# Indirect transfers of 126 rows in place of 125 in a graph network on one core: all five passes, the surplus row skipped

## The reference, cut to what matters

```python
edge_index = jnp.stack([src, dst])
h = relu(layernorm(x))
x = x + spline_conv(h, edge_attr_2, weight, root_w, root_b, edge_index)   # messages from h[src], summed at dst, mean over the degree, + h @ root_w.T + root_b
h = relu(layernorm(x))
x = x + gat_layer(h, edge_index, ...)   # 8 heads, softmax over the edges into a node and its self loop, then an MLP of 128, two layer norms
```

## Time and profile before

| what | us |
|---|---|
| median of 3 runs | 3404.45 (3403.78 to 3404.93) |
| the profiled execution | 3409.07 |
| its span, first to last instruction | 3406.9 |
| GpSimd busy | 2542.2 (75%), 2011 instructions |
| TensorE busy | 2036.6 (60%) |
| VectorE busy | 2020.0 (59%) |
| ScalarE busy | 789.4 (23%) |

### The profile page before, as it was taken

One profiled execution on the slowest core, in us unless ns is written; L12 is line 12 of the kernel. 1 busy time (PEld: TensorE's weight loads), 2 busy tenths in 40 slices (PEclk: granted clock), 3 DMA queues, 4 the chain that ended last, 5 costly groups with the idle time before them and its releaser, 6 DMA issues.

```text
span 3406.9 us, 31556 instructions
## 1 busy us (share of the span) xinstructions
PE 2036.6 (60%) x8829; PEld 1383.9 (41%) x8829; DVE 2020.0 (59%) x3417; ACT 789.4 (23%) x1511; POOL 2542.2 (75%) x2011
## 2 busy tenths in 40 slices
PE   2877777737776654564555065464461587887740
PEld 1554454525554443443443053353341244444420
DVE  5788878885666454444533034333348998798720
ACT  1332222213333221222222021121121022223210
POOL 8788888888888788887787777888850038888877
PEclk9888888877777776776676565566565788798765
DMA  2322222221212111111111011111110001111100
GB/s 57 85 70 70 67 71 65 46 64 31 50 39 53 32 36 34 41 34 29 35 29 29 11 24 21 27 25 22 23 17 0 30 15 23 37 27 27 33 10 10
DMA packets 116041, 123.16 MB, mean 36 GB/s; under 512 B 70597, under 2 KB 72618, under 8 KB 115941
## 3 DMA queue, kind: packets, MB, share of 16 engines
q0 software_dynamic: 64000, 30.57, 9.4%
q1 hardware_dynamic: 51940, 91.52, 8.4%
HBM read 59.51 MB, written 64.00 MB: 36 GB/s over the span
## 4 chain that ended last, share of the span: by engine, by line
POOL 67%; issue 19%; DVE 7%; PE 5%; ACT 0%; DMA 0%; POOLq 0%; DVEq 0%; ACTq 0%
POOL ring L411 45%; POOL x_table L433 14%; POOL out_rows L459 9%; DVE region L1443 2%; PE C L527 1%; PE V L745 1%; DVE region L1435 1%; PE V L515 1%; DVE region L1419 1%; DVE region L1101 1%; DVE region L1371 0%; DVE region L1394 0%; DVE region L1391 0%; PE C L745 0%; PE T L745 0%
## 5 line engine op out<-in xcount | busy, mean ns | idle before, releaser
L411 POOL DMA_INDIRECT ring<-in_x,index x800 | 1044.7, 1306 | 244.3 <-issue 243.7
L459 POOL DMA_INDIRECT out_rows<-ring,index_out x400 | 507.7, 1269 | 370.3 <-DVE ring L1242 250.0
L411 POOL DMA_INDIRECT ring<-x_table,index x400 | 494.0, 1235 | 124.4 <-issue 124.4
L433 POOL DMA_INDIRECT x_table<-region,index_out x400 | 492.8, 1232 | 121.9 <-issue 121.6
L476 PE MATMUL T<-ident,hrow 125*128 125x125 f32 x1000 | 198.9, 338 | 487.9 <-DVE hrow L1086 285.3
L527 PE MATMUL C<-w_c,hid 128*125 128x32 f32 x2400 | 354.9, 314 | 211.2 <-ACT hid L826 191.7
L1060 DVE TENSOR_REDUCE var<-sq 125x16 f32<-125x512 f32 x325 | 220.7, 682 | 375.8 <-ACT sq L810 284.4
L527 PEld LDWEIGHTS C<-w_c,hid 128*125 128x125 f32 x2400 | 351.2, 237 | 216.0 <-ACT hid L826 196.1
L515 PE MATMUL V<-xT,w_q 128*128 128x500 f32 x600 | 391.2, 809 | 63.8 <-ACT xT L802 38.7
L476 PEld LDWEIGHTS T<-ident,hrow 125*128 125x128 f32 x1000 | 150.4, 182 | 529.6 <-DVE hrow L1086 264.9
L1080 DVE TENSOR_REDUCE var<-ring 125x16 f32<-125x512 f32 x50 | 34.2, 684 | 497.1 <-DMA ring<-x_table,index 299.5
(11 more groups left out here) (229 smaller groups left out, 3192.3 us busy)
## 6 DMA issues: line engine op xcount, KB each, us to landing
ring<-in_x,index POOLq DMA_INDIRECT x800
nodes<-in_x SPq DMA_DIRECT2D x25, 500.0 KB
x_table<-nodes SPq DMA_DIRECT2D x25, 500.0 KB
x_plain<-nodes SPq DMA_DIRECT2D x25, 500.0 KB
nodes<-x_plain SPq DMA_DIRECT2D x50, 250.0 KB
out_rows<-nodes SPq DMA_DIRECT2D x50, 250.0 KB
x_table<-region,index_out POOLq DMA_INDIRECT x400
ring<-x_table,index POOLq DMA_INDIRECT x400
```

The lines of the kernel that those rows point to most:

```text
L411: pool.indirect_dma_start(out=ring[0:P, j, s * F:(s + 1) * F], out_offset=None, in_=table, in_offset=bass.IndirectOffsetOnAxis(ap=index[0: ...
L433: pool.indirect_dma_start(out=x1_table[:, :], out_offset=bass.IndirectOffsetOnAxis(ap=index_out[0:P, j, s:s + 1], axis=0), in_=rows_out[0: ...
L459: pool.indirect_dma_start(out=out[:, :], out_offset=bass.IndirectOffsetOnAxis(ap=index_out[0:P, j, s:s + 1], axis=0), in_=ring[0:P, j, s * ...
```

## The change

Every indirect transfer gets a 126th row. Its index is N, out of range, so nothing is moved for it; the gathers get the same bounds check that the scatters have. The indices of partition 125 on are set by VectorE at the start, `index` and `index_out` from partition 96 on (the loads and copies write partitions 0 to 124 over it later), and so is the part of `region2` from which row 125 of the scatters is addressed. `root_b` goes into rows 125 to 127 of `ring`, ahead of the first index load in SP's queue; GpSimd waits for it before its first gather and SP waits for the two index fills before its first index load. The centring of rows in SBUF by VectorE (`centre_rows`) is in the kernel before and stays as it is.

```diff
-N_BOOT = 6 * 4 + 2 + 2 + 2 + 4
+N_BOOT = 6 * 4 + 2 + 2 + 2 + 3
...
+ROWS = 126
...
+        index_set = sem("index_set"); root_b_in = sem("root_b_in")
...
+            sp.dma_start(ring[P:128, :, :].rearrange("a j (s f) -> a (j s) f", f=F),
+                         root_b.rearrange("(a b f) -> a b f", a=1, b=1).to_broadcast([128 - P, NJ * CE, F])).then_inc(root_b_in, 16)
+            sp.wait_ge(index_set, 2)
             for j in range(NJ):
                 index_load(src, 0, j, None)
...
-            load(ring[P:P + 1, :, :].rearrange("a j (s f) -> a (j s) f", f=F),
-                 root_b.rearrange("(a b f) -> a b f", a=1, b=1).to_broadcast([1, NJ * CE, F]))
...
             def gather(table, j):
...
-                        out=ring[0:P, j, s * F:(s + 1) * F], out_offset=None, in_=table,
-                        in_offset=bass.IndirectOffsetOnAxis(ap=index[0:P, j, s:s + 1], axis=0)).then_inc(ring_dma[j], 16)
+                        out=ring[0:ROWS, j, s * F:(s + 1) * F], out_offset=None, in_=table,
+                        in_offset=bass.IndirectOffsetOnAxis(ap=index[0:ROWS, j, s:s + 1], axis=0),
+                        bounds_check=last_row, oob_is_err=False).then_inc(ring_dma[j], 16)
...
+            pool.wait_ge(root_b_in, 16)
             gather_phase(x[:, :], 0, 0)
...
-                        out=x1_table[:, :], out_offset=bass.IndirectOffsetOnAxis(ap=index_out[0:P, j, s:s + 1], axis=0),
-                        in_=rows_out[0:P, j, s * F:(s + 1) * F], in_offset=None,
+                        out=x1_table[:, :], out_offset=bass.IndirectOffsetOnAxis(ap=index_out[0:ROWS, j, s:s + 1], axis=0),
+                        in_=rows_out[0:ROWS, j, s * F:(s + 1) * F], in_offset=None,
...
+            pool.wait_ge(index_set, 2)
...
-                            out=out[:, :], out_offset=bass.IndirectOffsetOnAxis(ap=index_out[0:P, j, s:s + 1], axis=0),
-                            in_=ring[0:P, j, s * F:(s + 1) * F], in_offset=None,
+                            out=out[:, :], out_offset=bass.IndirectOffsetOnAxis(ap=index_out[0:ROWS, j, s:s + 1], axis=0),
+                            in_=ring[0:ROWS, j, s * F:(s + 1) * F], in_offset=None,
...
+            v.memset(index[96:128, :, :], N).then_inc(index_set, 1)
+            v.memset(index_out[96:128, :, :], N).then_inc(index_set, 1)
+            v.memset(region2[96:128, 5904 + KS * GF:2 * H * TE + NJ * W], 0.0)
             dve.sem_inc(c_done, CREDIT)
```

## The result

The changed kernel takes 3898.07 us (3890.69 to 3907.39, 4 runs) against 3404.69 for the kernel before: 1.145 times as long, 95% interval 1.142 to 1.1475. I had forecast 2836.

A forecast was written before the change was run, and what follows sets the result against it. GpSimd's queue of 2,000 indirect transfers was taken to bound the kernel. From 3409.1, 492 saved through stage D and 78 in E, plus 2 for boot, gave 2841, or 2836 as median; range 2720 to 3200, chance 0.79.

The forecast's parts named there:

- VectorE keeps its times: Stage E, scatters to the output: VectorE's times stay, the last scatter lands at 3326 instead of 3404, 78 us saved.
- can go at 34.5: Stage B, dst gathers and x1 scatters: 34.5 us a chunk instead of 49.1, once VectorE no longer waits for the ring.
- VectorE's 118 a block: Stage A, first gathers: VectorE bounds at about 118 us per five-chunk block instead of 133.2, saving 60 us.
- my 0.83: Indirect transfer's instruction on GpSimd: 0.83 us instead of 1.21, the middle between 0.44 (all steps) and 1.21 or 1.22.
- my own table: Whole-kernel times for other instruction durations: 0.44 to 0.6 us gives 2745, 0.7 2775, 0.9 2925, 1.0 3055, 1.1 3205.
- Stage D: Gathers from the x1 table: 25 chunks take 464 us, ending at 2035 instead of 2527.5; 492 us saved in all.
- Rival 2: Transfer cost goes by rows, or by engines with rows: 1.22 us by rows, 3426 us in all; chance 0.10.
- slower: Whole kernel slower than before by over 0.2%: chance 0.10, against 0.85 for faster and 0.05 for the same.
- My signs of being wrong: Instruction over 1.0 us, the 0.30 us gap growing, or stage B above 40 us a chunk with GpSimd waiting.
- The gap of 0.30: Time on GpSimd between one indirect transfer and the next: stays 0.30 us, for a period of 1.13.
- The packets: Last stretch of scatters: 14 large and 18 small packets for each transfer, against 5 large and 27 small before.
- The bounds check: New on the gathers only; costed at nothing, at worst 0.02 us each, 24 us where GpSimd bounds.

The follow-up runs named there:

- 112 rows: Changed kernel with transfers of 112 rows, 7 on each of 16 engines, the rows beyond not moved: 3018.66 us on chip 5, 4060.79 on chip 8.
- 85 and 119 rows: Two changed kernels with 17 rows on each of 5 or 7 engines, rows beyond not moved, ring zeroed: 3350.48 and 3343.50 us.
- 49 rows: Changed kernel with transfers of 49 rows, 7 on each of 7 engines, the rows beyond not moved: 3077.82 us on chip 5, 3927.66 on chip 8.
- 105: Changed kernel with transfers of 105 rows, 7 on each of 15 engines, the rows beyond not moved: 3962.09 us on chip 3.
- 121 rows: Changed kernel with transfers of 121 rows, 11 on each of 11 engines, rows beyond not moved, ring zeroed: 3663.84 us.
- my first series: Changed kernel with fewer rows per transfer (85, 119, 121), rows beyond not moved, ring zeroed: 3350.48, 3343.50 and 3663.84 us.

## Why the prediction was wrong

*The step that failed* is in the working of the stages: "VectorE keeps its times", B that "can go at 34.5", A at VectorE's 118 a block. I took the pace of the other engines from rows in which GpSimd went at 1.51 us, and let it stand at 1.13. On the chips of the result their pace depends on GpSimd's: below a period somewhere between 1.47 us, where nothing is late, and 1.41 or 1.39, where it begins, TensorE's signals reach ScalarE and VectorE late, by 1 to 2.4 us on the mean in whole kernels. The instruction alone, 1.0 to 1.07 us in place of my 0.83, would by my own table have given 3055 to 3205 (112 rows, the nearest kernel without late signals, took 3019). By that estimate 690 to 840 us of the 3898 are this step. The second layer and the convolution are chains of short steps between TensorE and those two, so each delay is on the path. It feeds back: the late engines give `ring` and indices late, GpSimd waits (B's 391 us), and in its pauses the signals are prompt. So a shorter instruction buys GpSimd nothing. Stage D shows it best: its mean period is 1.43 to 1.55 us in every late kernel, against 1.54 before, though the median goes down to 1.29.

*Was this in the rows before?* No row of it showed a late signal, and none of my rivals had it. Rival 2, the one on the slower side, had "14 engines cost more to serve than 5", but at the price of GpSimd's own instruction, which did fall. So the 0.10 that I gave to "slower" would have been right by luck and not by its reason. My signs of being wrong did catch it: B is at 52 us a chunk (1300/25) with GpSimd waiting, and the instruction is above 1.0 us.

*The transfer.* The mechanism was right and its size off. Steps count: (1.190 - 0.987)/16 = 0.0127 us each for the scatter. But 25 of them are 0.32 of the 1.19 us; the other 0.87 is fixed. 17 steps took 1.082, 11 took 1.024 and 7 took 0.942 to 0.964, within 0.02 of that line, and 85 and 119 rows, both of 17 steps, took the same time, so it is the steps and not the rows. I had taken the middle of the bounds, 0.83, and the scatter measured 0.987, the gather 1.071. The gap of 0.30 held. The Trainium skill, "DMA: Bandwidth & Descriptors", section "Anatomy of one DMA — SWDGE (gpsimd) path", has the descriptors as a small part. By these runs they are about a quarter of the instruction at 125 rows: less than the half of my middle, but not nothing. The scatter came out about halfway between my 0.83 and the unchanged 1.19 of that rule. The packets fell out as expected from the divisor: 32 for each transfer still, and in the last stretch (3800 to 3880 us, 49 transfers) 14 large and 18 small.

*The bounds check* was costed at nothing or 0.02 us. It is 0.06 on each gather (72 us in all), and 0.078 in D at 126 rows, there with the skipped row. The scatters, on which I based it, have it in both kernels, so their equal time could not tell.

*The rest of the sum* can be judged where the signals are prompt. On chip 5 VectorE is 95% busy in stage A (381.77 of 400), and 400 gathers take 562 us, 22.5 a chunk where I had put 23.6. B, from first scatter to D, takes 955; my own steps with its period of 1.27 (gathers 1.29, scatters 1.25) give 847 + 720 x 0.14 = 948. D's gathers take 521 against 25 x 16 x 1.33 = 532. My table gave 3055 for an instruction of 1.0 us; 112 rows (0.99 and 0.94) took 3019, 49 rows (1.03 and 0.955) 3078. By that table 126 rows would take between 3055 and 3205 on that chip, an estimate: they were not run there.

*What stays open.* The traces show what is late and when, not which part of the chip delays it. Two things could stand behind "chip 5". No chip was used twice, so what I call the chip could be anything else that held for that group of runs. And one more thing marks chip 5: only there is every update recorded. A gather raises its semaphore 16 times; the trace has all 16 on chip 5 in stage A (15.9 to 16.0), and 12.4 of them in the kernel before and in the kernels of the same stage A elsewhere. As far as the results show, every execution here was recorded in this way, so it is not tested whether the recording itself has a part in the delay.

With the updates of the other DMAs the numbers are these: in stage A, where the two kernels with only stage D changed have the same code as the kernel before, the trace holds 18.6 records of DMAs updating semaphores for each gather on chip 5 and 14.7 on chip 3 as in the trace of before. After the change it is 7.7, at 112 rows on chip 8 5.4, on chip 5 18.6. They are few where signals are late, though not in strict order (with eight increments 5.5, at a lateness of 0.62). That fits updates of DMAs and of TensorE meeting at one place, but is not a proof, and fewer records can be lost records. Updates as such are not it: GpSimd's own sixteen more for each transfer, at 1.77 us, left TensorE's prompt. Why VectorE's and ScalarE's own signals stay prompt, and whether the number of engines adds something at one period, I can't say (49 rows at 1.34: 1.82; 105 at 1.35: 1.90, on two chips). Nor does the period alone set the size: at 121 rows gathers come every 1.41 us in A and in D, and lateness counted by stage is 0.93 in A and 0.24 in D.

No version here beats the kernel before on the chips with the effect with all rows moved. 126 rows in D alone give 2.5% on chip 5, and with the check nothing on chip 3 (+0.6%). Without the check it was not run on a chip with the effect; its period, 1.30, lies where signals were late.

## What to carry to other kernels

An engine's time in a trace is measured beside the others at their present pace. When a change speeds up the stream of small transfers in the background, ask whether the handoffs between the other engines still hold; a "remote" releaser on a single core, growing in every consumer of one engine, is the sign that its signals are late. Try the same program on more than one chip before a few per cent are believed, and vary rate and size apart: my first series changed both.

Before a row is added to make a divisor larger, price what skips it: the check of bounds alone cost more than 2% here.

## What was not expected of the hardware

- Indirect transfers every 1.29 to 1.41 us delayed TensorE's signals by 1 to 2.4 us on the mean, single ones by over 25, on every chip seen but one; gathers every 1.47 us or more did not (0.03 in the stages that have only those).
- One chip, or something else about its one group of runs, was without it: the same program took 3018.66 us there and 4060.79 on another, with the kernel before alike to 1 us.
- An indirect scatter costs GpSimd 0.87 us and 0.0127 for each row on an engine; a gather with a check of bounds costs 0.06 us more than one without.
- Eight semaphore increments behind a transfer left the median gap at 0.305 us, sixteen made it 0.70 to 0.78.
